# Last output chunk's rounding behind the last convolution's boundary, relation stage's first tables read in the gated block, root sums around the low parts

## The chip, the cores and the metric

The program runs on one core of one Trainium2 chip. TensorE (PE in the rows) multiplies, VectorE (DVE), ScalarE (ACT) and GpSimd (POOL) do the rest, and SyncE (SP) and ScalarE's own queue start DMAs. The engines run side by side and meet only at semaphores; each takes its own instructions in the order in which they are written. The metric is the device time of the whole program in microseconds (us), as a median of runs; lower is better.

## What is computed

Four layers on 256 nodes of 768 features, each a graph part and a feed-forward part added to the node stream x. The change lies in the gated feed-forward part of layer 2 (eight experts, one chosen) and in layer 3: a relational graph convolution, a plain one behind it, and a feed-forward part with two of eight experts. All data is fp32.

```python
# layer 3, graph part (x is already normalised)
agg  = segment_sum(x[src], edge_type * n + dst, 34 * n)
cnt  = segment_sum(ones,   edge_type * n + dst, 34 * n)
mean = agg.reshape(34, n, -1) / maximum(cnt, 1).reshape(34, n, 1)
h1   = einsum('rni,rio->no', mean, W_rel) + x @ W_root + b_rgcn
xw   = h1 @ W_gcn
out  = segment_sum(xw[src] * norm, dst, n) + xw * dinv**2 + b_gcn     # added to x
# layer 3, feed-forward part (on the normalised x)
probs  = softmax(x @ Wr + br); weights of the two largest, scaled to sum 1
h      = gelu(x @ W1[e] + b1[e]) for 8 experts
out    = sum_e weight_e * (h_e @ W2[e] + b2[e]); layer norm; added to x
```

## The kernel before, in words

**Precision by parts.** An fp32 product is made of three passes of TensorE: hi*hi, lo*hi and hi*lo. So every weight chunk that SyncE loads into `w_in` is first rounded by ScalarE into `w_hi` (`high`, `high_chunk`), and then VectorE writes the remainder into `w_lo` (`low`, `low_chunk`, through `low_of`). Both buffers have two halves, used in turn; each chunk goes in two parts p = 0 and 1, of three row tiles each. `w_in` has one buffer for each p: SyncE starts the load of the next chunk's part p when ScalarE and VectorE have both counted the part before (`w_high[p]`, `w_low[p]`). TensorE waits for `w_low` (`chunk`, `weights`).

**A boundary.** Between two parts the stream x is updated from PSUM, its statistics are taken (`stats_of`), it is scaled into `xn` (the memory of `neg_b`), TensorE turns it (`turn_tile`), ScalarE rounds the turned tile (`evict_tile`, with the square root of the variance before it in `deviation`) and VectorE writes its remainder (`low_tile`). There are two tiles m = 0 and 1 of 128 nodes. `boundary` does this for the convolutions' outputs, `tile_by_tile` is ScalarE's side of it.

**The gated block and the relation stage.** In the gated block of layer 2, ScalarE rounds and VectorE lowers the chunk C_ROOT, VectorE adds the block's output to x (`gated_out`), and the boundary to the relation stage follows. TensorE multiplies by `W_root` (`product` into REL_BANKS, tiles 0 and 1). Then, for each of 34 relations, a 256x256 table of edge counts is read from HBM into `ct` (the memory of `scores_b`) by a DMA on ScalarE's queue (`load_counts`, two half buffers). VectorE clips it into `REL_C[half]`, which is `aT_hi` or `aT_lo` (`counts`, semaphore `r_count`). TensorE forms the transposed means out of it (`mean`, banks 3 to 5), ScalarE rounds these (`round_means`, semaphore `r_high`), VectorE writes the remainder (`mean_low`, semaphore `r_low`: `hid_lo` for even relations, `xT_lo` for odd ones), and TensorE multiplies by the relation's weights (`relation`). The product of the relation before lies in the same banks, so `relation` waits for `r_acc`, which VectorE counts when it has taken a tile's sum out: `root(m)` for the root product, `accumulate(r, m)` for a relation. TensorE's order at the entry is: root product of tile 0, of tile 1, `mean(0, 0)`, seven filling matmuls (`idle`), `relation(0)`.

**The last convolution.** `gcn(1)` multiplies by `W_gcn` and aggregates; VectorE's `gcn_out(1)` is the boundary 8 behind it. TensorE then turns tile 0, multiplies by the chunk C_FFN3, scores the router (8 columns wide) and goes on. The chunks C_FFN3 + 1 and + 2 (`ffn_out` in the rows, 97 partitions) are needed only by the last products.

**What sets the order.** Nothing is planned by a tool: each engine's program is written by hand in the order in which it runs. So an instruction that stands too early in a list holds back all that stands behind it.

Of the kernel before, what the change touches and what calls it, by code (L numbers as in the profile page):

```python
# [16 lines left out]
P = 128  # L17
N = 256
# [43 lines left out]
def gnn_ffn_kernel(nc, t):  # L62

    ctx = ExitStack()
    with ctx:
# [180 lines left out]
        def flat(ap):  # L246
            return ap.rearrange("p a b -> p (a b)")
# [616 lines left out]
        def _(act):  # L864
# [243 lines left out]
            high_chunk(C_ROOT)  # L1108
            for m in range(M):
                act.wait_ge(*((f_mm[2], 5) if m == 0 else (w_used, used(C_FFN2 + 2))))  # L1110
                for (b, c0, c1, o) in NODE_BANKS[m]:
                    keep(outb[:, m, o:o + c1 - c0], bank[b][:, c0:c1], f_act[2])
                if m == 0:
                    deviation(0)
# [4 lines left out]
            act.wait_ge(e_added, 16 * ET + 16)  # L1119

            def load_counts(r, half):
                act.dma_start(ct[:, half, :, :], table[bass.ds(r * N, N), :].rearrange("(m p) n -> p m n", p=P))\
                   .then_inc(ld_ct[half], 16)

            load_counts(0, 0)
            load_counts(1, 1)
# [33 lines left out]
            high_chunk(C_FFN3 + 1)  # L1160


            tile_by_tile(8)
            act.wait_ge(f_dve[3], 1)
# [11 lines left out]
        def _(dve):  # L1176
# [418 lines left out]
            low_chunk(C_ROOT)  # L1595
            dve.wait_ge(x_type, 1)
# [16 lines left out]
            biased(3)  # L1613
            dve.wait_ge(x_high, 1)
            low_of(h_lo[:, :, :], xn[:, :, :], h_hi[:, :, :], x_low)

            def counts(half, landed):

                dve.wait_ge(ld_ct[half], landed)
                ts(flat(REL_C[half][:, :, :]), flat(ct[:, half, :, :]), EXACT, ALU.min).then_inc(r_count, 1)  # L1620
# [33 lines left out]
            counts(0, 16)  # L1654
            low(nth(C_REL), 0)
            mean_low(0, 0)
            counts(1, 16)
            for m in range(M):
                root(m)
                dve.wait_ge(r_acc, m + 1)  # L1660
            low(nth(C_REL) + 1, 1)
            accumulate(0, 0)
            mean_low(1, 1)
            with dve.Fori(1, REL // 2) as i:
                for half in range(2):
                    r = i * 2 + half
                    counts(half, i * 16 + 16)
                    dve.wait_ge(r_acc, r * 2 - 1)
                    accumulate(r - 2, 1)
                    low(r + nth(C_REL), half)  # L1670
                    accumulate(r - 1, 0)
                    mean_low(r, half)
# [19 lines left out]
            low_chunk(C_FFN3 + 1)  # L1692
            gcn_out(1)


            route(3)
# [82 lines left out]
```

## Time and profile before

| | us |
|---|---|
| median of 3 runs | 1414.98 (1413.61 to 1418.78) |
| the profiled execution | 1413.81 |
| its span, from the first to the last instruction | 1412.0 |
| TensorE matmul busy | 1307.5 (93%) |
| VectorE busy | 1004.7 (71%) |
| ScalarE busy | 627.4 (44%) |
| mean granted clock of TensorE | 0.981 of 2.4 GHz |

Times in rows are counted from the first instruction of the span. A row of the timeline has the start, the duration (of several merged instructions together), the engine, the line, what is written and read, and in brackets the idle time ahead of it and who ended it. An engine that ends in q is the engine's queue, which starts DMAs. A busy TensorE is not TensorE at full speed: its clock is granted at 2.4 or 1.2 GHz (1.00 or 0.50 in the rows).

### The profile page before, as it was taken

The numbers are of one execution on the slowest core, as the hardware profiler recorded it, in microseconds if no ns is written. First come the engines' busy times: TensorE is split into PE (matmuls) and PEld (weight loads), VectorE is DVE, ScalarE is ACT, GpSimd is POOL, SyncE is SP. The second block draws the span as 40 slices with busy tenths as digits, with TensorE's granted clock in tenths as the row PEclk, the third lists the DMA queues.
The fourth block names the chain that finished last, engine by engine and source line by source line (L and its number), as shares of the span: only waits on it lengthen the run. The fifth ranks groups of instructions, "written<-read, shape, count | busy, mean of one in ns | idle before, by whom it ended". The sixth has DMA issues, their size and how long they took to land.

```text
span 1412.0 us, 21374 instructions
## 1 busy us (share of the span) xinstructions
PE 1307.5 (93%) x7833; PEld 1145.5 (81%) x7833; DVE 1004.7 (71%) x1677; ACT 627.4 (44%) x795; POOL 216.0 (15%) x160
## 2 busy tenths in 40 slices
PE   5799999997899999997899999999999999999876
PEld 4499999974689999976677788888898889889765
DVE  7888888877798888876857756665665566566555
ACT  2256665544355665543444434333433333343421
POOL 0033444331024334440000000000000000002000
PEclk9999999998999999999999999999999999999988
DMA  9465556653266655643334544454445445434610
GB/s 345 147 200 195 163 163 191 202 132 92 87 194 200 184 163 164 201 148 112 116 109 156 192 181 149 159 199 162 149 178 193 149 150 195 175 141 146 197 36 23
DMA packets 103718, 227.32 MB, mean 161 GB/s; under 512 B 16688, under 2 KB 34672, under 8 KB 103684
## 3 DMA queue, kind: packets, MB, share of 16 engines
q1 hardware_dynamic: 72780, 192.43, 38.5%
q10 hardware_dynamic: 20968, 31.78, 8.0%
q0 software_dynamic: 9936, 2.66, 1.9%
q8 instruction: 20, 0.33, 0.1%
q14 instruction: 14, 0.11, 0.0%
HBM read 216.56 MB, written 10.29 MB: 161 GB/s over the span
## 4 chain that ended last, share of the span: by engine, by line
PE 63%; DVE 24%; issue 8%; ACT 3%; DMA 1%; DVEq 1%; ACTq 0%; SPq 0%
PE bank L418 61%; DVE w_lo L1181 6%; DVE hid_lo L1181 2%; DVE h_lo L1181 2%; DVE neg_b L1325 1%; DVE scores_b L1276 1%; DVE stats L1219 1%; ACT w_hi L892 1%; DVE scores_b L1278 1%; DVE scores_b L1187 1%; ACT z_b L960 1%; PE bank L457 1%; PE bank L514 1%; DVE same L1299 1%; DVE spare L1394 1%
## 5 line engine op out<-in xcount | busy, mean ns | idle before, releaser
L1181 DVE TENSOR_TENSOR w_lo<-w_in,w_hi 128x2304 fp32r<-128x2304 f32 (+4 forms) x162 | 396.5, 2476 | 61.4 <-ACT w_hi L892 61.3
L892 ACT ACTIVATE w_hi<-w_in 128x2304 fp32r<-128x2304 f32 (+4 forms) x162 | 328.4, 2062 | 234.7 <-PE bank L418 197.2
L418 PE MATMUL bank<-w_hi,xT_hi 128*128 128x384 f32 (+3 forms) x942 | 323.4, 343 | 7.0 <-DVE xT_lo L1181 4.5
L418 PE MATMUL bank<-w_lo,xT_hi 128*128 128x384 f32 (+3 forms) x942 | 308.8, 340 | 0.0
L418 PE MATMUL bank<-w_hi,hid_hi 128*128 128x512 f32 (+2 forms) x858 | 294.6, 343 | 9.0 <-DVE hid_lo L1181 3.5
L418 PE MATMUL bank<-w_lo,hid_hi 128*128 128x512 f32 (+2 forms) x858 | 272.5, 338 | 0.0
L418 PE MATMUL bank<-w_hi,xT_lo 128*128 128x384 f32 (+3 forms) x942 | 247.3, 341 | 0.0
L418 PE MATMUL bank<-w_hi,hid_lo 128*128 128x512 f32 (+2 forms) x858 | 225.2, 339 | 0.0
L418 PEld LDWEIGHTS bank<-w_hi,xT_hi 128*128 128x128 f32 (+1 forms) x942 | 178.2, 189 | 36.4 <-issue 8.9
L418 PEld LDWEIGHTS bank<-w_hi,hid_hi 128*128 128x128 f32 (+1 forms) x858 | 162.3, 189 | 45.5 <-issue 4.7
L1641 DVE SCALAR_TENSOR_TENSOR neg_b<-bank,rinv,neg_b 128x512 f32<-128x512 f32 (+1 forms) x136 | 77.5, 611 | 157.5 <-PE bank L418 157.5
L418 PEld LDWEIGHTS bank<-w_lo,xT_hi 128*128 128x128 f32 (+1 forms) x942 | 177.9, 189 | 13.8 <-issue 0.8
L418 PEld LDWEIGHTS bank<-w_lo,hid_hi 128*128 128x128 f32 (+1 forms) x858 | 162.5, 189 | 18.9
L377 POOL DMA_INDIRECT table<-value,row_i x64 | 121.6, 1899 | 255.1 <-DMA table<-value,row_i 236.7
L418 PEld LDWEIGHTS bank<-w_hi,xT_lo 128*128 128x128 f32 (+1 forms) x942 | 157.2, 190 | 2.4 <-issue 0.8
L418 PEld LDWEIGHTS bank<-w_hi,hid_lo 128*128 128x128 f32 (+1 forms) x858 | 134.7, 191 | 1.0
L418 PE MATMUL bank<-aT_hi,h_hi 128*128 128x256 f32 (+1 forms) x408 | 106.4, 280 | 2.7 <-DVE aT_lo L1181 2.7
L418 PE MATMUL bank<-aT_hi,h_lo 128*128 128x256 f32 (+1 forms) x408 | 106.7, 283 | 0.0
L418 PE MATMUL bank<-aT_lo,h_hi 128*128 128x256 f32 x396 | 103.9, 281 | 0.0
L892 ACT ACTIVATE xT_hi<-bank 128x512 fp32r<-128x512 f32 (+1 forms) x87 | 46.6, 554 | 119.5 <-PE bank L418 65.2
L403 POOL DMA_INDIRECT w_in<-L_gnn_W_rel,xrow_i x6 | 7.3, 1212 | 531.0 <-DVE w_lo L1181 529.5
L1187 DVE CUSTOM_DVE_ANT_0 spare<-z_b,a_bc 128x768 f32<-128x768 f32 x72 | 69.0, 958 | 20.6 <-ACT z_b L892 12.4
(225 smaller groups left out, 1565.2 us busy)
## 6 DMA issues: line engine op xcount, KB each, us to landing
w_in<-L_gnn_W_rel SPq DMA_DIRECT2D x68, 1152.0 KB, 5.6
w_in<-L_gnn_W SPq DMA_DIRECT2D x66, 1152.0 KB, 5.7
table<-zrow SPq DMA_DIRECT2D x1, 9216.0 KB, 36.2
scores_b<-table ACTq DMA_DIRECT2D x34, 256.0 KB, 2.9
a_bc<-L_gnn_a_src ACTq DMA_DIRECT2D x18, 384.0 KB, 3.8
a_bc<-L_gnn_a_dst ACTq DMA_DIRECT2D x18, 384.0 KB, 5.3
key_row<-key_rows ACTq DMA_DIRECT2D x16, 256.0 KB, 5.5
w_in<-ffn_out SPq DMA_DIRECT2D x4, 864.0 KB, 7.0
```

The source lines that it names most:

```text
L377: pool.indirect_dma_start(out=cells, out_offset=bass.IndirectOffsetOnAxis(ap=row_i[:, g:g + 1], axis=0), in_=value[:, g:g + 1], in_offset= ...
L418: return pe.matmul(out, lhsT, rhs, start=start, stop=stop, **kw)
L457: last = pe.transpose(bank[TURNED[i][m][half]][:, k * P:(k + 1) * P], xn[:, m, (3 * half + k) * P:(3 * half + k + 1) * P], ident[:, :])
L514: last = pe.transpose(bank[7][:, sm * N + m * P:sm * N + (m + 1) * P], alpha[:, m, sm * P:(sm + 1) * P], ident[:, :])
L892: act.activation(out, ps, func, **kw).then_inc(mark, 1)
L960: last = act.activation(z_b[:, k, :], bank[(5, 3, 4)[j]][:, (k % 2) * N:(k % 2 + 1) * N], ACT.Identity, bias=b1_head[:, k:k + 1])
L1181: return dve.tensor_tensor(out, a, b, op)
L1187: return dve.tensor_tensor_reduce(out=out, in0=a, in1=b, scale=1.0, scalar=0.0, op0=op0, op1=op1, accum_out=acc)
L1219: last = dve.bn_stats(stats[:, m, j, :], x_sb[:, m, j * HALF:(j + 1) * HALF])
L1276: last = dve.scalar_tensor_tensor(score[:, m, :], bank[7][:, 0:N], scal[:, 2 + m:3 + m], mask[:, m, :], add_, add_)
L1278: step(dve.scalar_tensor_tensor(flat(leaky[:, :, :]), flat(score[:, :, :]), 0.2, flat(score[:, :, :]), mul, mx))
L1641: last = dve.scalar_tensor_tensor(xs, bank[b][:, c0:c1], weight, xs, mul, add_)
```

## The change

Three groups of instructions move within the lists of ScalarE and VectorE; TensorE's and SyncE's lists stay as they are, and no instruction is added or removed.

1. ScalarE reads the first two count tables behind the rounding of C_ROOT instead of behind `h_hi`, and VectorE clips both directly behind the remainders of C_ROOT.
2. At the entry of the relation stage VectorE does `root(0)` ahead of the first relation's weight remainders and `root(1)` behind them, ahead of `mean_low(0, 0)`; `biased(3)`, which adds a bias to x, moves behind `mean_low(1, 1)`.
3. ScalarE rounds C_FFN3 + 1 behind both tiles of boundary 8, and VectorE lowers it behind `gcn_out(1)`.

```diff
@@ ScalarE
             high_chunk(C_ROOT)
+            act.wait_ge(e_added, 16 * ET + 16)
+            def load_counts(r, half):
...
+            load_counts(0, 0)
+            load_counts(1, 1)
...
             keep(h_hi[:, :, :], xn[:, :, :], x_high)
-            act.wait_ge(e_added, 16 * ET + 16)
...
-            load_counts(0, 0)
-            load_counts(1, 1)
...
-            high_chunk(C_FFN3 + 1)
             tile_by_tile(8)
+            high_chunk(C_FFN3 + 1)
@@ VectorE
             low_chunk(C_ROOT)
+            counts(0, 16)
+            counts(1, 16)
             dve.wait_ge(x_type, 1)
...
             low_tile(6, 1)
-            biased(3)
             dve.wait_ge(x_high, 1)
             low_of(h_lo[:, :, :], xn[:, :, :], h_hi[:, :, :], x_low)
...
-            counts(0, 16)
+            dve.wait_ge(x_low, 1)
+            root(0)
             low(nth(C_REL), 0)
+            root(1)
             mean_low(0, 0)
-            counts(1, 16)
-            for m in range(M):
-                root(m)
-                dve.wait_ge(r_acc, m + 1)
+            dve.wait_ge(r_acc, 2)
             low(nth(C_REL) + 1, 1)
             accumulate(0, 0)
             mean_low(1, 1)
+            biased(3)
...
             gcn_low(1)
+            gcn_out(1)
             low_chunk(C_FFN3 + 1)
-            gcn_out(1)
             route(3)
```

VectorE's list at the entry of the relation stage, before: behind the last tile's remainder come the two bias additions, `h_lo`, the first clipped table (`aT_hi`), the remainders of the first relation's weights, those of its means, the second table, and the root sums (`neg_b` from `hbias_bc`).

```order
L1181 TENSOR_TENSOR x_sb<-x_sb,bias_bc 128x768 [waits ld_bias]
L1181 TENSOR_TENSOR x_sb<-x_sb,bias_bc 128x768
L1181 TENSOR_TENSOR h_lo<-neg_b,h_hi 128x1536 [waits x_high,dve_step]
L1184 TENSOR_SCALAR aT_hi<-scores_b 128x512 [waits ld_ct0]
L1181 TENSOR_TENSOR w_lo<-w_in,w_hi 128x2304 [waits w_high_0]
L1181 TENSOR_TENSOR w_lo<-w_in,w_hi 128x2304 [waits w_high_1]
L1181 TENSOR_TENSOR hid_lo<-bank,hid_hi 128x512 [waits rel_high] x3
L1184 TENSOR_SCALAR aT_lo<-scores_b 128x512 [waits ld_ct1]
L1181 TENSOR_TENSOR neg_b<-bank,hbias_bc 128x512 [waits rel_out]
L1181 TENSOR_TENSOR neg_b<-bank,hbias_bc 128x256
L1181 TENSOR_TENSOR neg_b<-bank,hbias_bc 128x512 [waits w_used,rel_acc]
L1181 TENSOR_TENSOR neg_b<-bank,hbias_bc 128x256
```

The same place of the changed kernel.

```order
L1181 TENSOR_TENSOR h_lo<-neg_b,h_hi 128x1536 [waits x_high]
L1181 TENSOR_TENSOR neg_b<-bank,hbias_bc 128x512 [waits rel_out,x_low]
L1181 TENSOR_TENSOR neg_b<-bank,hbias_bc 128x256
L1181 TENSOR_TENSOR w_lo<-w_in,w_hi 128x2304 [waits w_high_0]
L1181 TENSOR_TENSOR w_lo<-w_in,w_hi 128x2304 [waits w_high_1]
L1181 TENSOR_TENSOR neg_b<-bank,hbias_bc 128x512 [waits w_used]
L1181 TENSOR_TENSOR neg_b<-bank,hbias_bc 128x256
L1181 TENSOR_TENSOR hid_lo<-bank,hid_hi 128x512 [waits rel_high] x3
```

The root sums stand ahead of the mean's remainders, the two tables have left the stretch, and so have the bias additions.

ScalarE's list in the gated block, as a piece of the difference: `w_hi` is the rounding of C_ROOT, `spare` takes the block's output from PSUM.

```order
 L892 ACTIVATE w_hi<-w_in 128x2304 [waits w_full_0,w_used]
 L892 ACTIVATE w_hi<-w_in 128x2304 [waits w_full_1]
+L1112 DMA scores_b<-table 128x2x256 [waits e_added]
+L1112 DMA scores_b<-table 128x2x256
 L892 ACTIVATE spare<-bank 128x512 [waits ffn2_mm]
 L892 ACTIVATE spare<-bank 128x256
```

The two table reads now stand between the last rounding of C_ROOT and the first eviction of the block's output.

ScalarE's list at boundary 8, as a piece of the difference: `std` and `xT_hi` are the boundary's two tiles, the rows of 97 partitions the chunk C_FFN3 + 1.

```order
 L892 ACTIVATE rw_hi<-rw 128x48 [waits ld_mid]
+L892 ACTIVATE std<-mv 128x1 [waits ln_var]
+L892 ACTIVATE xT_hi<-bank 128x3x128 [waits ln_t] x2
+L892 ACTIVATE std<-mv 128x1 [waits ln_var]
+L892 ACTIVATE xT_hi<-bank 128x3x128 [waits ln_t] x2
 L892 ACTIVATE w_hi<-w_in 97x2304 [waits w_row_0,w_full_0,w_used]
 L892 ACTIVATE w_hi<-w_in 97x2304 [waits w_row_1,w_full_1]
```

The boundary's six activations stand ahead of the chunk's two roundings; on VectorE the chunk's two remainders go in the same way from ahead of the boundary's first `x_sb` to behind its last `xT_lo`, ahead of the router's first instruction.

## Rows read from the trace of the kernel before

**Rows 1.** Timeline, VectorE, from the gated block's end to the relation stage's entry.
```profile
752.26 5.03 DVE L1181 TENSOR_TENSOR w_lo<-w_in,w_hi 128x2304 fp32r<-128x2304 f32 x2 [1.22 <-ACT w_hi L892]
...
769.21 1.82 DVE L1181 TENSOR_TENSOR x_sb<-x_sb,bias_bc 128x768 f32<-128x768 f32 x2
771.06 1.76 DVE L1181 TENSOR_TENSOR h_lo<-neg_b,h_hi 128x1536 fp32r<-128x1536 f32 x1
...
776.08 5.03 DVE L1181 TENSOR_TENSOR w_lo<-w_in,w_hi 128x2304 fp32r<-128x2304 f32 x2 [2.92 <-ACT w_hi L892]
781.02 1.88 DVE L1181 TENSOR_TENSOR hid_lo<-bank,hid_hi 128x512 fp32r<-128x512 f32 x3
782.82 0.41 DVE L1184 TENSOR_SCALAR aT_lo<-scores_b 128x512 fp32r<-128x512 f32 x1
783.15 2.07 DVE L1181 TENSOR_TENSOR neg_b<-bank,hbias_bc 128x512 f32<-128x512 f32 x4
```

**Rows 2.** Timeline, TensorE, same stretch: turn, root product, first mean, first relation.
```profile
761.05 0.87 PE L457 MATMUL bank<-ident,neg_b 128*128 128x128 f32 x6 [1.14 <-DVE neg_b L1184]
...
767.22 0.82 PE L457 MATMUL bank<-ident,neg_b 128*128 128x128 f32 x6
...
776.31 0.28 PE L418 MATMUL bank<-aT_hi,h_hi 128*128 128x256 f32 x1
...
784.22 0.50 PE L418 MATMUL bank<-w_hi,hid_hi 128*128 128x512 f32 x1 [3.34 <-DVE neg_b L1181]
```

**Rows 3.** Timeline, ScalarE and its queue, same stretch.
```profile
768.08 0.39 ACTq L1122 DMA_DIRECT2D scores_b<-table  x1
...
768.50 1.49 ACT L892 ACTIVATE h_hi<-neg_b 128x1536 fp32r<-128x1536 f32 x1
...
773.92 4.15 ACT L892 ACTIVATE w_hi<-w_in 128x2304 fp32r<-128x2304 f32 x2 [3.92 <-DVE aT_hi L1184]
...
779.39 0.60 ACT L892 ACTIVATE hid_hi<-bank 128x512 fp32r<-128x512 f32 x1 [0.35 <-PE bank L418]
```

**Rows 4.** Table reads: time from issue to landing of all 34.
```profile
DMA to landing us min/median/max: 2.6/2.9/4.3
```

**Rows 5.** Stretches: length, busy time (count) by engine, granted clock, DMA share, GB/s.
```profile
785.80:788.80 3.00, 3.00 (x11) 2.52 (x10) 2.49 (x1) 2.15 (x2) 0.00 (x0) 0.50 0.43 154
...
1354.40:1359.40 5.00, 4.99 (x17) 3.85 (x18) 2.96 (x7) 1.07 (x3) 0.00 (x0) 0.52 0.02 3
```

**Rows 6.** Timeline, VectorE, one turn of the relation loop.
```profile
817.17 1.14 DVE L1641 SCALAR_TENSOR_TENSOR neg_b<-bank,rinv,neg_b 128x512 f32<-128x512 f32 x2 [4.78 <-PE bank L418]
```

**Rows 7.** Timeline, VectorE, behind the last convolution.
```profile
1347.53 2.56 DVE L1181 TENSOR_TENSOR w_lo<-w_in,w_hi 97x2304 fp32r<-97x2304 f32 x1 [1.06 <-ACT w_hi L892]
1350.00 1.14 DVE L1544 SCALAR_TENSOR_TENSOR x_sb<-bank,dinv,x_sb 128x512 f32<-128x512 f32 x2
```

**Rows 8.** Timeline, TensorE, behind the last convolution.
```profile
1343.48 1.90 PE L418 MATMUL bank<-zero 128*128 128x512 bf16 x8
1354.41 1.54 PE L457 MATMUL bank<-ident,neg_b 128*128 128x128 f32 x6 [9.03 <-DVE neg_b L1184]
...
1362.04 0.82 PE L457 MATMUL bank<-ident,neg_b 128*128 128x128 f32 x6
```

**Rows 9.** Timeline, VectorE and TensorE, behind layer 2's convolution.
```profile
716.09 1.14 DVE L1544 SCALAR_TENSOR_TENSOR x_sb<-bank,dinv,x_sb 128x512 f32<-128x512 f32 x2 [1.29 <-PE bank L418]
...
716.94 1.90 PE L418 MATMUL bank<-zero 128*128 128x512 bf16 x8
720.50 0.88 PE L457 MATMUL bank<-ident,neg_b 128*128 128x128 f32 x6 [1.66 <-DVE neg_b L1184]
```

**Rows 10.** Timeline, ScalarE and VectorE, boundary 8's second tile, router, hidden sums.
```profile
1362.57 0.88 ACT L892 ACTIVATE xT_hi<-bank 128x384 fp32r<-128x384 f32 x2 [6.00 <-PE bank L457]
...
1368.90 0.17 DVE L1181 TENSOR_TENSOR lg<-bank,rb 128x16 f32<-128x16 f32 x1 [4.79 <-PE bank L418]
...
1376.87 1.02 DVE L1181 TENSOR_TENSOR z_b<-bank,hbias_bc 128x512 f32<-128x512 f32 x2 [1.93 <-PE bank L418]
```

More of the change, by code:

```diff
@@ L1108, in _ @@
             high_chunk(C_ROOT)
+            act.wait_ge(e_added, 16 * ET + 16)
+            def load_counts(r, half):
+                act.dma_start(ct[:, half, :, :], table[bass.ds(r * N, N), :].rearrange("(m p) n -> p m n", p=P))\
+                   .then_inc(ld_ct[half], 16)
+            load_counts(0, 0)
+            load_counts(1, 1)
             for m in range(M):
@@ L1118, in _ @@
             keep(h_hi[:, :, :], xn[:, :, :], x_high)
-            act.wait_ge(e_added, 16 * ET + 16)
-            def load_counts(r, half):
-                act.dma_start(ct[:, half, :, :], table[bass.ds(r * N, N), :].rearrange("(m p) n -> p m n", p=P))\
-                   .then_inc(ld_ct[half], 16)
-            load_counts(0, 0)
-            load_counts(1, 1)
             def round_means(r, half, more):
@@ L1159, in _ @@
             keep(rw_hi[:, :], rw[:, :], rw_high)
+            tile_by_tile(8)
             high_chunk(C_FFN3 + 1)
-            tile_by_tile(8)
             act.wait_ge(f_dve[3], 1)
@@ L1595, in _, with counts @@
             low_chunk(C_ROOT)
+            def counts(half, landed):
+                dve.wait_ge(ld_ct[half], landed)
+                ts(flat(REL_C[half][:, :, :]), flat(ct[:, half, :, :]), EXACT, ALU.min).then_inc(r_count, 1)
+            counts(0, 16)
+            counts(1, 16)
             dve.wait_ge(x_type, 1)
@@ L1612, in _ @@
             low_tile(6, 1)
-            biased(3)
             dve.wait_ge(x_high, 1)
             low_of(h_lo[:, :, :], xn[:, :, :], h_hi[:, :, :], x_low)
-            def counts(half, landed):
-                dve.wait_ge(ld_ct[half], landed)
-                ts(flat(REL_C[half][:, :, :]), flat(ct[:, half, :, :]), EXACT, ALU.min).then_inc(r_count, 1)
             def excess(landed):
```

## The prediction

> **What bounds the kernel now.** The first look is at the table of busy shares: TensorE works for 93% of the span and its list is unchanged, so time can only come out of stretches in which TensorE waits or runs at the lower clock. The second look is at the timeline of the two places that the change touches. At the entry of the relation stage TensorE has finished the first mean and its filling matmuls, then idles 3.34 us until VectorE's `neg_b`, the root sums [rows 2]. VectorE works without a break in that time: 5.03 us of weight remainders, 1.88 us of mean remainders, a table, 2.07 us of root sums [rows 1]. Behind the last convolution TensorE idles 9.03 us [rows 8]; there VectorE sits in front of the remainders of C_FFN3 + 1, whose last part ends at 1350.09, and only then does the boundary begin, at 1350.00 (the starts of neighbours overlap a little) [rows 7]. The third look is at the granted clock in both places: after each of the two waits it reads about one half for a while, 0.50 over 3.0 us and 0.52 over 5.0 us [rows 5]. So each wait costs twice: once as idle time, once as slow matmuls behind it.
>
> **The change part by part**, with times of the profiled execution.
>
> *Tables in the gated block.* VectorE clips both tables directly behind the remainders of C_ROOT, which end at 757.29 [rows 1]. One takes 0.41 us, and its follower starts 0.33 us after it [rows 1], so the two cost about 0.7 us. VectorE is the engine that TensorE waits for in the boundary that follows (1.14 us at 761.05 [rows 2]), so nothing hides this: **+0.7 us** for all that comes behind, the root product and the first mean included. The tables must have landed by 757.29. ScalarE's queue runs ahead of its engine: a read that is written behind `h_hi` was issued at 768.08, while `h_hi` started at 768.50 [rows 3]. In the gated block the read stands behind a rounding that waits for the root weights; VectorE's first remainder starts at 752.26 and the second rounding soon after, so I put the issue at 752.6 and 753.1. Landing takes 2.6 to 4.3 us [rows 4]: the second table is there between 755.7 and 757.4. I take the median, 2.9, so no wait; the upper end costs 0.1 us, and a read that has to share with the weights' load might add 1 us. The Trainium skill, DMA: Bandwidth & Descriptors, section Issuing engines are not separate DMA queues, says that reads started by ScalarE interleave with SyncE's on the same 16 engines, which speaks against reading tables where weights stream in; by it the landing would tend to the upper end, and the sum would lose those tenths. ScalarE itself pays for the issues in its queue only, not in its engine.
>
> *Relation entry.* With the 0.7 us the first mean starts at 777.0 instead of 776.31 [rows 2]. Before, ScalarE began its last rounding of the mean 3.08 us after that start (779.39 [rows 3]). Now: 780.1, 0.60 us long, 0.3 us to VectorE, 0.7 us for the last remainder, which makes **781.7**. The other path to the same point is VectorE's own list. `h_hi` ends at 770.0 + 0.7 [rows 3]; `h_lo` takes 1.76, `root(0)` half of 2.07, the weight remainders 5.03, `root(1)` 1.04, the mean remainders 1.88 [rows 1]: with 0.2 for the first hand-over this gives 781.6. The weight remainders are not late any more: ScalarE's rounding of them was held until 773.92 by the wait for the first table [rows 3], which stood behind the biases (1.82 us) and `h_lo` (1.76 us) on VectorE [rows 1]; the table is now clipped long before, so the rounding starts right behind `h_hi`, at 770.7, and the first part is done at 772.8, before VectorE asks for it at 773.7. `root(1)` asks at 778.7 for a product that is done at 777.0. So TensorE starts `relation(0)` at 781.7 instead of 784.22: **-2.5 us**, the 0.7 paid already. The filling matmuls now end about there, so the gap of 3.34 us shrinks to some tenths.
>
> *The clock behind it.* Without the gap I expect the clock to stay at 1.00, as it does after the gap of 1.14 us at 761.05. The 3.0 us at 0.50 [rows 5] then take 1.5: **-1.5 us**.
>
> *Biases.* 1.82 us [rows 1], now between `mean_low(1, 1)` and the loop, where VectorE has 4.78 us of idle time in each turn [rows 6]. What is queued behind is the clipping of relation 2's table, needed only a product later. **0 us.** The same slack of 4.78 us says that the loop is bound by TensorE, so what the entry gains goes through all 34 relations unchanged.
>
> *Boundary 8.* In layer 2 the same convolution has no rounding ahead of its boundary: VectorE starts on the sum 0.85 us before the first filling matmul behind the aggregation (716.09 against 716.94 [rows 9]). Here these fillers start at 1343.48 [rows 8], so VectorE can start at 1342.6 instead of 1350.00: **-7.4 us**. From there to the turn it takes 4.41 us in both layers (1350.00 to 1354.41, 716.09 to 720.50 [rows 7 to 9]), and nothing else becomes late: VectorE and ScalarE have nothing left ahead of it. TensorE's gap is then 1.7 us as in layer 2 [rows 9] instead of 9.03.
>
> *The clock behind that.* From the turn of tile 0 to that of tile 1 TensorE took 7.63 us here (1354.41 to 1362.04 [rows 8]) and 6.17 us for the same instructions in boundary 6 (761.05 to 767.22 [rows 2]), where the clock had stayed up: **-1.5 us**.
>
> *Where the rounding goes.* ScalarE rounds behind `xT_hi` of tile 1, which ends at 1363.45 [rows 10]; 2.1 us for the first part (half of 4.15 [rows 3]), 0.3 to VectorE, two remainders in 5.0 us: 1370.9 in the old times, against 1368.90 for the router's first instruction [rows 10]. The router's chain is 2.0 us late. But behind it VectorE waited 1.93 us for TensorE before the hidden sums of tile 1 [rows 10]: the lateness takes this wait's place, and **+0.1 us** is left. The last chunk's load starts later too, but its rounding stands behind the hidden sums of 1376.87 [rows 10].
>
> **The sum**: -2.5 - 1.5 - 7.4 - 1.5 + 0.1 = -12.8 us. The profiled execution would take 1413.81 - 12.8 = 1401.0, the median 1414.98 - 12.8 = 1402.2. A measurement of this kernel can tell about 0.5%, 7 us, from no change.
>
> **The rivals.**
>
> *The clock falls all the same.* The gaps of 1.7 us at boundary 8, of 1.8 us now at boundary 6, or what is left at the relation entry might bring it down in one or two places, or the router's narrow matmuls might do it longer than before. For it: there is one row at 1.7 us, in layer 2, and none at 1.8 in boundary 6. Against: in that row the clock stayed up. Price: 1.5 us for each place, so **1403.7 to 1405.2**. The Trainium skill, TensorE: Matmul & The Clock Gate, Part 1: The HAM clock gate, says that the monitor runs on without regard to the kernel, so the point at which the clock changes moves from run to run; by that rule a shift of the whole stream alone can win or lose such a stretch.
>
> *The rounding that was moved becomes the wait.* If ScalarE comes to the chunk late, or the two remainders take the router's place by more than the 1.93 us of slack, each us beyond is lost one to one: the whole of the 5.0 us of remainders less 1.93 is the most that this can take, 3.1 us, **1405.3**.
>
> *It doesn't do what it says at boundary 8.* If VectorE can't start on the sum before 1350 for another reason (the sum's banks, ScalarE), only the entry's 4.0 us are left: **1411**. Layer 2's rows speak against it.
>
> *Slower.* The relation loop starts at another phase against the loads of weights and tables, and the turn, bound by TensorE so far, becomes bound by VectorE's or the loads' chain. It decides from 12.8 / 33 = 0.39 us a turn; at 0.6 us a turn the time is 1402.2 + 33 x 0.6 = **1422**. Against it: all waits in the loop hang on the turn itself, with 4.78 us to spare [rows 6].
>
> **How the numbers follow.** The forecast, 60%: 1402.2, from 1400.5 to 1403.5. The clock falls in one or two places, 22%. The rounding becomes the wait, 10%. Only the entry gains, 4%. Slower, 2%; the last 2% is left to gains beyond the sum, such as a stretch of low clock behind the router that goes too. The range must also hold the spread of the runs, 1413.61 to 1418.78 for the kernel before, so it goes from 1399.0 to 1406.5. Faster by over 0.5% needs 1407.9 or less: 0.94. Within 0.5%: 0.04. Slower: 0.02.
>
> **What would show it.** In the timeline of the changed kernel: two clippings of 0.4 us directly behind the remainders of C_ROOT with no wait for a DMA ahead of them; a gap of TensorE before the first relation under 1 us and a clock of 1.00 over the 10 us behind it; the turn of boundary 8 about 3.5 us behind the start of the eight filling matmuls instead of 10.9; the two remainders of 97 partitions ahead of the router's first instruction; and VectorE's wait ahead of the second hidden sum gone. It would be wrong if VectorE showed a wait for a table, if the clock read 0.50 in either place, or if the loop's turn were no longer the same length.

## The result, and the profile after

| | before | after |
|---|---|---|
| median, same chip | 1416.25 us (1413.61 to 1419.41, 6 runs) | 1405.49 us (1403.43 to 1407.49, 6 runs) |
| ratio | | 0.9914, 95% interval 0.9901 to 0.9928 |
| profiled execution | 1413.81 us | 1407.49 us |
| its span | 1412.0 us | 1405.7 us |
| granted clock, mean | 0.981 | 0.980 |

The changed kernel is faster by 10.8 us in the medians. The forecast was 12.8 us and 1402.2, counted from a median of 1414.98 before; more runs of the kernel before put that at 1416.25. The two medians alone give a ratio of 0.9924, inside the interval.

The two spans differ by 6.3 us only, and yet the change was worth more than that. VectorE's remainders of C_ROOT, its last work that is the same in both kernels, start at 752.26 before [rows 1] and at 755.70 after. Instructions are the same up to there; what differs is TensorE's granted clock in some stretches. One of them, in the kernel before and then in the changed one (columns as in [rows 5]):

```profile
704.00:707.40 3.40, 3.40 (x21) 3.01 (x20) 3.37 (x4) 3.40 (x5) 0.00 (x0) 1.00 0.59 119
```

```profile
704.00:707.40 3.40, 3.40 (x13) 2.82 (x12) 3.37 (x5) 3.34 (x4) 0.00 (x0) 0.50 0.51 119
```

TensorE is busy all the time in both, with 21 matmuls in one and 13 in the other. Over all traces of this study whose code is the same up to there, C_ROOT's remainders start anywhere from 751.93 to 757.10. So from here on two traces are compared from that start, called R below, and not by their spans. From R to the end the kernel before takes 659.74 us and the changed one 649.98: the change is worth **9.8 us in the trace**. R has an uncertainty of its own: in some traces the second half of `W_root` lands a little later, and all behind R with it, by up to 0.4 us.

The entry of the relation stage, VectorE of the changed kernel (timeline), answers to [rows 1]:

```profile
755.70 5.03 DVE L1181 TENSOR_TENSOR w_lo<-w_in,w_hi 128x2304 fp32r<-128x2304 f32 x2 [1.22 <-ACT w_hi L892]
760.65 0.42 DVE L1184 TENSOR_SCALAR aT_hi<-scores_b 128x512 fp32r<-128x512 f32 x1
760.98 0.42 DVE L1184 TENSOR_SCALAR aT_lo<-scores_b 128x512 fp32r<-128x512 f32 x1
...
775.93 1.02 DVE L1181 TENSOR_TENSOR neg_b<-bank,hbias_bc 128x512 f32<-128x512 f32 x2
776.87 5.01 DVE L1181 TENSOR_TENSOR w_lo<-w_in,w_hi 128x2304 fp32r<-128x2304 f32 x2
781.80 1.01 DVE L1181 TENSOR_TENSOR neg_b<-bank,hbias_bc 128x512 f32<-128x512 f32 x2
782.73 2.09 DVE L1181 TENSOR_TENSOR hid_lo<-bank,hid_hi 128x512 fp32r<-128x512 f32 x3
```

Both clippings stand behind the remainders with no bracket, so no wait for a table: the two reads were issued at 756.0 and 756.4 and landed 2.7 and 2.9 us later, over a microsecond ahead of the clippings. The wait of 2.92 us ahead of the relation's weight remainders [rows 1] is gone. TensorE, same stretch, answers to [rows 2]:

```profile
765.17 0.88 PE L457 MATMUL bank<-ident,neg_b 128*128 128x128 f32 x6 [1.81 <-DVE neg_b L1184]
...
780.42 0.28 PE L418 MATMUL bank<-aT_hi,h_hi 128*128 128x256 f32 x1
...
783.30 1.68 PE L418 MATMUL bank<-zero 128*128 128x512 bf16 x7
785.16 0.49 PE L418 MATMUL bank<-w_hi,hid_hi 128*128 128x512 f32 x1 [0.17 <-issue]
```

The idle time ahead of `relation(0)` fell from 3.34 to 0.17 us. Boundary 8, TensorE with VectorE's first sum among it, answers to [rows 7] and [rows 8]:

```profile
1338.57 0.57 PE L418 MATMUL bank<-h_hi,cntT_hi 128*128 128x512 f32 x1 [1.82 <-DVE h_lo L1181]
...
1343.57 1.14 DVE L1544 SCALAR_TENSOR_TENSOR x_sb<-bank,dinv,x_sb 128x512 f32<-128x512 f32 x2 [4.03 <-PE bank L418]
...
1344.42 1.90 PE L418 MATMUL bank<-zero 128*128 128x512 bf16 x8
1347.99 0.88 PE L457 MATMUL bank<-ident,neg_b 128*128 128x128 f32 x6 [1.66 <-DVE neg_b L1184]
...
1354.07 0.82 PE L457 MATMUL bank<-ident,neg_b 128*128 128x128 f32 x6
```

The gap of 9.03 us is 1.66. Stretches of the changed kernel: behind `relation(0)`, the last aggregation, the turn of boundary 8, and behind the router.

```profile
784.20:794.20 10.00, 9.83 (x63) 8.44 (x62) 7.19 (x6) 5.39 (x4) 0.00 (x0) 1.00 0.69 248
...
1338.60:1344.50 5.90, 5.90 (x25) 4.96 (x26) 1.87 (x4) 0.00 (x0) 0.00 (x0) 0.71 0.92 215
...
1344.40:1354.00 9.60, 7.43 (x42) 5.21 (x41) 6.29 (x15) 1.16 (x4) 0.00 (x0) 1.00 0.00 0
...
1359.30:1366.10 6.80, 6.80 (x28) 6.22 (x28) 6.00 (x19) 2.98 (x4) 0.00 (x0) 0.50 0.30 88
```

Both low stretches of [rows 5] are at 1.00 now. Two others took part of the gain: the last aggregation at 0.71, which the kernel before did at 1.00, and a longer low stretch behind the router. The aggregation in the kernel before, timeline and stretch:

```profile
1339.16 0.50 PE L418 MATMUL bank<-h_hi,cntT_hi 128*128 128x512 f32 x1 [1.80 <-DVE h_lo L1181]
```

```profile
1339.20:1345.10 5.90, 5.90 (x32) 4.32 (x32) 2.13 (x3) 2.13 (x1) 0.00 (x0) 1.00 0.83 201
```

The same gap of 1.8 us stands ahead of it in both kernels; in one the clock fell behind it, in the other not.

Marks from R, in us, for the kernel before and the changed one:

| from R to | before | after | difference | so far forecast |
|---|---|---|---|---|
| turn of boundary 6 | 8.79 | 9.47 | +0.68 | +0.7 |
| `relation(0)` | 31.96 | 29.46 | -2.50 | -2.5 |
| the next mean, behind `relation(0)` | 39.89 | 35.86 | -4.03 | -4.0 |
| last aggregation | 586.90 | 582.87 | -4.03 | -4.0 |
| turn of boundary 8, tile 0 | 602.15 | 592.29 | -9.86 | -11.4 |
| the same, tile 1 | 609.78 | 598.37 | -11.41 | -12.9 |
| turn of the hidden values (`spare` by `ident`), behind router and hidden sums | 629.21 | 619.44 | -9.77 | -12.8 |
| end | 659.74 | 649.98 | -9.76 | -12.8 |

### The profile page after: what moved, and what is told of

The parts are those of the page before. It is cut to its first block, busy times and chain, and to the rows that moved or that the text cites. A ratio compares the mean times of both kernels' runs of the same rounds, so it can differ in the third digit from the quotient of the medians.

```text
span 1405.7 us, 21373 instructions
## 1 busy us (share of the span) xinstructions
PE 1310.6 (93%) x7833; PEld 1149.2 (82%) x7833; DVE 1004.6 (71%) x1677; ACT 627.4 (45%) x795; POOL 217.0 (15%) x160
## 4 chain that ended last, share of the span: by engine, by line
PE 61%; DVE 24%; issue 8%; ACT 4%; DMA 1%; DVEq 1%; ACTq 0%; SPq 0%
PE bank L418 59%; DVE w_lo L1181 6%; DVE hid_lo L1181 2%; DVE h_lo L1181 2%; DVE neg_b L1325 1%; ACT w_hi L892 1%; DVE scores_b L1276 1%; DVE stats L1219 1%; DVE scores_b L1278 1%; ACT z_b L960 1%; DMA w_in<-L_gnn_W 1%; DVE scores_b L1187 1%; PE bank L457 1%; DVE same L1299 1%; PE bank L514 1%
```

## The experiments

The question that the traces leave: is each term what the prediction says, and are the 3 us that are missing in the last table lost to the clock or to the moved rounding? The rival says that the rounding, which now stands ahead of the router, costs them. Every kernel below computes the whole; filling matmuls multiply zeros and add nothing to the result.

**The halves.** The entry alone is the changed kernel with boundary 8 as before:

```diff
 ScalarE                          VectorE
+high_chunk(C_FFN3 + 1)          +low_chunk(C_FFN3 + 1)
 tile_by_tile(8)                  gcn_out(1)
-high_chunk(C_FFN3 + 1)          -low_chunk(C_FFN3 + 1)
```

> The changes at the gated block and at the relation entry alone; boundary 8 as before. My theory: two independent places, whose gains add. The first relation starts 2.5 us earlier, measured from the start of C_ROOT's remainders (31.96 before, 29.5 now), the clock behind it stays at 1.00 (1.5 us), boundary 8 keeps its wait of 9.0 us: 2.5 to 4.0 us faster, ratio 0.9972 to 0.9982. Rival (one place is swallowed by the other, or the gain of the entry is given back in the relation loop): ratio 1.000, with a turn of the loop longer than 15.51 us.

Measured: 1415.07 us, ratio 0.9986 (0.9974 to 0.9998). `relation(0)` starts at R + 31.38, only 0.58 earlier than before, and not the expected 2.5. From the turn of boundary 6 it is 21.53 against 19.99 in the changed kernel, and 1.5 of this stand between the root product and the first mean (14.91 us here, 13.38 before). Timeline of TensorE and the stretch behind it:

```profile
764.72 0.88 PE L457 MATMUL bank<-ident,neg_b 128*128 128x128 f32 x6 [2.55 <-DVE neg_b L1184]
```

```profile
766.80:770.10 3.30, 3.30 (x11) 2.82 (x11) 2.10 (x6) 0.20 (x1) 0.00 (x0) 0.50 0.02 5
```

The clock fell during the root product, behind the turn's gap of 2.55 us. The turn itself is 0.38 later than in the changed kernel, R + 9.85, because the second half of `W_root` landed later. The mean behind `relation(0)` is at R + 37.78, 2.11 earlier than before: the 4.03 of the changed kernel less 1.5 for the low stretch and 0.4 for the turn. Behind the loop 0.6 us of this are lost again: the clock fell in the last aggregation, and the turn of boundary 8 comes 15.57 us behind the aggregation's start instead of 15.25.

The other half is the kernel before with only the boundary's edits:

```diff
 ScalarE                          VectorE
-high_chunk(C_FFN3 + 1)          -low_chunk(C_FFN3 + 1)
 tile_by_tile(8)                  gcn_out(1)
+high_chunk(C_FFN3 + 1)          +low_chunk(C_FFN3 + 1)
```

> The change at boundary 8 alone. My theory: TensorE's wait there falls from 9.0 to 1.7 us, 7.4 us faster, and 1.5 us more by the clock: 7.4 to 8.9 us, ratio 0.9937 to 0.9948, and with e1_entry's gain it makes the whole of the change. Rival (the remainders that now stand ahead of the router's first instruction cost up to 3.1 us): 4.3 us or more, ratio 0.997, with no wait of VectorE left ahead of the second hidden sum.

Measured: 1411.65 us, 0.9959 (0.9946 to 0.9973). From the last aggregation to the turn 7.88 us instead of 15.25: -7.37, the term of -7.4. The next turn follows 6.08 instead of 7.63 us later: -1.55. And then 1.6 us are lost behind the router, as in the changed kernel (18.27 us from the router's first matmul to the turn of the hidden values, 16.68 before). In the timeline VectorE waits ahead of the second hidden sum as long as before [rows 10], where the forecast had said that this wait would be gone; the stretch shows why:

```profile
1374.30 1.02 DVE L1179 TENSOR_TENSOR z_b<-bank,hbias_bc 128x512 f32<-128x512 f32 x2 [1.99 <-PE bank L418]
```

```profile
1363.50:1370.30 6.80, 6.80 (x25) 6.12 (x26) 5.93 (x21) 2.61 (x3) 0.00 (x0) 0.50 0.32 88
```

TensorE is busy for all of it, at 0.50. VectorE waits for a slow TensorE, not TensorE for the late rounding.

**Parts of the entry.** The tables alone are read and clipped in the gated block; roots and biases stay:

```diff
 ScalarE:  high_chunk(C_ROOT)
+          load_counts(0, 0); load_counts(1, 1)
 VectorE:  low_chunk(C_ROOT)
+          counts(0, 16); counts(1, 16)
```

> Only the first two tables are read and clipped in the gated block; root sums and bias additions stay where they were. By VectorE's list: the clippings cost 0.7 us ahead of the boundary, the weights' rounding is no longer held by a table, and the root sums behind the mean's remainders still hold TensorE: first relation 30.6 us behind the start of C_ROOT's remainders (31.96 before, 29.5 with the whole change), a gain of 1.4 us. Rival (the table held nothing of the path): 0.7 us later than before.

Measured: 1415.67 us, 0.9986 (0.9971 to 1.0002), which can't be told from no change by the median. By the trace, from the turn to `relation(0)` 20.61 instead of 23.17 us; less 0.68 for the clippings ahead of the turn, this is -1.9 us. From R it starts at 30.46 (expected 30.6). TensorE in the timeline:

```profile
787.56 0.50 PE L418 MATMUL bank<-w_hi,hid_hi 128*128 128x512 f32 x1 [0.81 <-DVE neg_b L1181]
```

The gap is 0.81 and the relation behind it runs at full clock: 6.42 us to the next mean instead of 7.93.

The counterpart moves `root(0)`, `root(1)` and `biased(3)` and leaves the tables:

```diff
-biased(3)
 low_of(h_lo, xn, h_hi)
 counts(0, 16)
+root(0)
 low(nth(C_REL), 0)
+root(1)
 mean_low(0, 0)
...
 mean_low(1, 1)
+biased(3)
```

> Only the order at the entry: biases behind the second mean's remainders, root sums around the weight remainders; both tables are read and clipped where they were. By VectorE's list: the rounding of the weights still waits for the first table, now clipped 1.8 us earlier for want of the biases; first relation 31.2 us behind the start of C_ROOT's remainders, a gain of 0.7 to 0.8 us. Rival (the root sums are the whole of the wait): 29.9 us, a gain of 2.1 us.

Measured: 1416.54 us, 0.9988 (0.9971 to 1.0004). From the turn to `relation(0)` 22.07 us, -1.1; from R 31.24, as expected (31.2), and not the rival's 29.9. VectorE still waits for the weights' rounding, which the first table's clipping still holds back, and TensorE still waits for the mean's remainders:

```profile
777.12 5.03 DVE L1181 TENSOR_TENSOR w_lo<-w_in,w_hi 128x2304 fp32r<-128x2304 f32 x2 [2.00 <-ACT w_hi L892]
```

```profile
785.21 0.49 PE L418 MATMUL bank<-w_hi,hid_hi 128*128 128x512 f32 x1 [2.29 <-DVE hid_lo L1181]
```

With a gap of 2.29 the relation is slow (7.99 us). So each part alone helps, and in these traces only the ones with the tables moved have a gap small enough (1.00 us or less) that the clock stays.

Back in the changed kernel, the biases return to their old place:

```diff
 low_tile(6, 1)
+biased(3)
 low_of(h_lo, xn, h_hi)
...
 mean_low(1, 1)
-biased(3)
```

> The changed kernel with the two bias additions (1.82 us) back in their old place ahead of h_lo. By VectorE's list: h_lo waited 0.73 us for ScalarE in the changed kernel, so 1.82 - 0.73 = 1.1 us reach the list, and the first relation starts 0.8 to 1.1 us later than in the changed kernel (30.3 to 30.6 us). Rival (another path is as long): 29.5 us, no loss.

Measured: 1406.56 us, 0.9924 (0.9901 to 0.9946). `relation(0)` starts 0.84 us later (20.83 against 19.99 from the turn), as expected, with a gap of 1.00, and the relation is fast (6.40):

```profile
783.58 0.49 PE L418 MATMUL bank<-w_hi,hid_hi 128*128 128x512 f32 x1 [1.00 <-DVE hid_lo L1181]
```

All the same this trace ends at R + 649.20, 0.8 us before the changed kernel's: the aggregation stayed at full clock (1.5 us less) and so did more of the part behind the router (1.6 us less), while the product behind boundary 8's turn was slow (7.63 instead of 6.08 us). The clock's stretches are worth more than this part of the change.

**The price of the clippings ahead of the boundary.** In the changed kernel both move behind the scaling of the boundary's second tile:

```diff
 low_chunk(C_ROOT)
-counts(0, 16); counts(1, 16)
...
 scaled(1)
+counts(0, 16); counts(1, 16)
 low_tile(6, 1)
```

> The changed kernel with the two clippings moved from ahead of the boundary to behind the scaling of its second tile, where VectorE waits 2.7 us for ScalarE. My theory (the clippings sit on the path ahead of the boundary and cost 0.66 us there): the turn of boundary 6 and all behind it come 0.66 us earlier, the first relation 28.8 us behind the start of C_ROOT's remainders; ratio 0.0005 below the changed kernel's, which only the traces can show. Rival (something else sets the boundary): no difference in the trace.

Measured: 1407.14 us, 0.9929 (0.9906 to 0.9952). The turn is at R + 8.80 and `relation(0)` at R + 28.79, both 0.67 earlier than in the changed kernel. Timeline: the turn, and the clippings and the remainders behind them, which wait for ScalarE:

```profile
763.85 0.88 PE L457 MATMUL bank<-ident,neg_b 128*128 128x128 f32 x6 [1.13 <-DVE neg_b L1184]
```

```profile
768.28 0.42 DVE L1184 TENSOR_SCALAR aT_hi<-scores_b 128x512 fp32r<-128x512 f32 x1
768.62 0.42 DVE L1184 TENSOR_SCALAR aT_lo<-scores_b 128x512 fp32r<-128x512 f32 x1
...
771.06 1.02 DVE L1181 TENSOR_TENSOR xT_lo<-bank,xT_hi 128x384 fp32r<-128x384 f32 x2 [2.02 <-ACT xT_hi L892]
```

Ahead of these remainders VectorE waits for ScalarE in any case: 2.69 us in the changed kernel, and 2.02 here, where the clippings fill the rest. So they cost nothing there. That shows the +0.7 as a real price at their present place. A median can't show 0.67 us.

**What the clock gives back by itself.** If the waits cost a second time through the clock, then filling them with matmuls, and leaving their lengths, should give back that part alone. The kernel before, with the waits filled:

```diff
-idle(7, 7)
+idle(7, 21)
...
-turn_tile(8, 0, 8)
+turn_tile(8, 0, 48)
```

> The kernel before with more filling matmuls in the two waits of TensorE and nothing else changed: 21 instead of 7 ahead of the first relation, 48 instead of 8 ahead of boundary 8's turn. The waits for VectorE stay. My theory (a wait costs twice, as idle time and as slow matmuls behind it): the first relation and the turn start at the same distance as before, but the clock behind them reads 1.00; 3.0 us faster, ratio 0.998. Rival (the clock falls by the phase of the stream, not by these gaps): it reads 0.50 behind them as before, ratio 1.000.

Timeline of TensorE, the relation's start and the two turns of boundary 8:

```profile
786.25 0.50 PE L418 MATMUL bank<-w_hi,hid_hi 128*128 128x512 f32 x1 [0.33 <-DVE neg_b L1181]
...
1355.52 0.88 PE L457 MATMUL bank<-ident,neg_b 128*128 128x128 f32 x6 [0.97 <-DVE neg_b L1184]
...
1361.61 0.82 PE L457 MATMUL bank<-ident,neg_b 128*128 128x128 f32 x6
```

`relation(0)` starts as late as before from the turn (23.16 us), and its product takes 6.43 instead of 7.93; from turn to turn at boundary 8 it takes 6.09 (1361.61 - 1355.52) instead of 7.63. So in this trace the low clock behind the two waits went with the idle time, 1.5 us each. From R to the end it is 2.06 us shorter, and not 3.0: the turn of boundary 6 came 0.4 us later, where the second half of `W_root` landed later, and at boundary 8 the last chunk's load took 7.15 us instead of 6.59, so that the turn comes 0.6 us later behind the aggregation. But the timed runs say 1416.2 us, 1.0003 (0.9991 to 1.0014): at most 1.3 us faster (0.0009 x 1416). The expected gain is not in the median. The profiled run was the fastest of twelve, with the highest granted clock, 0.985; their median has 0.982 (1416.2 us), and the slowest 0.978 (1420.14 us). Where the other executions ran slowly no trace shows; that stays open.

Now the changed kernel itself, twice more, unchanged:

> The changed kernel again, unchanged. My theory: the waits are the same to 0.1 us, and the profiled executions differ in where the clock is at 0.50 in the boundaries with gaps of 1.6 to 1.9 us (in the first trace: ahead of the change and in the last aggregation). Expected: first relation 29.5 us behind the start of C_ROOT's remainders, turn of boundary 8 3.6 us behind the start of the fillers; total of the 0.50 stretches not the same as in the first trace; ratio 0.990 to 0.993. Rival (the low clock in the last aggregation and the longer one behind the router are caused by the change): they are in this trace at the same places again.

> The changed kernel a third time. My theory: the low stretch in the aggregation again, 9.4 us from its first matmul to the turn; ratio 0.9925, some 2 us above e11_aggfill2. Rival (chance): 7.9 us in this trace, and no difference between the two medians.

Measured: 1406.8 us, 0.9939 (0.9922 to 0.9956), and 1408.38 us, 0.9931 (0.9909 to 0.9953). The first of these repeats lies on the changed kernel's trace to within 0.03 us at nearly every mark, low stretches included, and ends at R + 649.96. That is what the rival had said, and not the expectation. The second repeat has some low stretches elsewhere. Its stretches, the last aggregation and the product behind boundary 8's turn:

```profile
1339.90:1345.80 5.90, 5.88 (x25) 4.98 (x26) 1.87 (x4) 0.00 (x0) 0.00 (x0) 0.71 0.91 208
...
1350.80:1354.20 3.40, 3.06 (x9) 2.61 (x10) 1.41 (x4) 0.08 (x1) 0.00 (x0) 0.50 0.02 5
```

The aggregation is slow again, now the turn's product is too (7.49 us instead of 6.09), and in exchange the part behind the router isn't (16.68 us instead of 18.31). It ends at R + 649.76, the same to 0.2 us.

So is the low clock in the aggregation a side effect of the change? The gap of 1.8 us ahead of it stands in eleven traces. In the five whose relation entry is that of the changed kernel (its three traces, the entry alone, the clippings late) the clock fell behind it. In the other six (before, boundary alone, tables alone, roots and biases alone, waits of before filled, biases back) it stayed. Chance alone would hardly sort them so. What in the entry does it, its shift of the stream or something else, no run separates.

To see what the aggregation's gap of 1.8 us is worth, seven more filling matmuls go into it in the changed kernel:

```diff
-idle(AGG_BANKS[1][0][0], 0 if sm else 2)
+idle(AGG_BANKS[1][0][0], 0 if sm else (9 if s else 2))
```

> The changed kernel with 9 instead of 2 filling matmuls ahead of the last aggregation, nothing else. My theory: TensorE's gap of 1.82 us there shrinks to 0.3, the clock reads 1.00 over the aggregation, the end of the aggregation comes 1.5 us earlier. Rival (the position of the stream against the monitor sets it, not this gap): the stretch of 0.50 is in the aggregation all the same or comes in the boundary right behind it.

Measured: 1404.47 us, 0.9907 (0.9885 to 0.9929). Timeline of TensorE ahead of the aggregation and at the second turn, VectorE at the router and the second hidden sum, and the stretch of the aggregation:

```profile
1337.07 0.50 PE L418 MATMUL bank<-h_hi,cntT_hi 128*128 128x512 f32 x1 [0.31 <-DVE h_lo L1181]
...
1351.03 0.82 PE L457 MATMUL bank<-ident,neg_b 128*128 128x128 f32 x6
...
1359.42 0.17 DVE L1181 TENSOR_TENSOR lg<-bank,rb 128x16 f32<-128x16 f32 x1
...
1365.86 1.02 DVE L1181 TENSOR_TENSOR z_b<-bank,hbias_bc 128x512 f32<-128x512 f32 x2 [0.41 <-PE bank L418]
```

```profile
1337.10:1343.00 5.90, 5.90 (x32) 4.32 (x32) 3.34 (x8) 0.00 (x0) 0.00 (x0) 1.00 0.89 213
```

The aggregation is at 1.00, from it to the turn 7.88 us instead of 9.42, and the part behind the router takes 16.68 us. This trace ends at R + 646.77, 12.97 us before the kernel before: the forecast's sum, in a trace in which the clock did what the forecast assumed, with seven matmuls that the change doesn't have. It also settles whether the rounding's lateness reaches TensorE. The router's first sum comes 8.39 us behind the turn of tile 1 (1359.42 - 1351.03), before 6.86 (1368.90 [rows 10] less 1362.04 [rows 8]): the moved rounding makes it 1.53 us late. The second hidden sum comes 14.83 us behind that turn in both (1365.86 - 1351.03, 1376.87 - 1362.04): the wait of 1.93 us has shrunk to 0.41 and taken all of it up.

Whether the moved rounding draws out the low stretch behind the router is another question. The part from the router's first matmul to the turn of the hidden values takes 16.7 us in all five traces with the old order. Of the nine with the new order it takes 18.2 to 18.3 in four (the changed kernel's first two, the boundary alone, the nine waits filled) and 16.7 in five. In those four the low stretch begins 2.5 to 3.6 us behind the router's first matmul and lasts 6.8 us, in the ten others it begins 4.0 to 5.2 us behind it and lasts 3.5. So the new order doesn't force the longer stretch; whether it makes it likelier, five traces of the old order can't tell.

The same kernel again:

> e10_aggfill once more, on one chip with e12_again2. My theory (the gap of 1.8 us, not chance, makes the low stretch in the aggregation): none in the aggregation, 7.9 us from its first matmul to boundary 8's turn; ratio to before 0.9905. Rival (chance from trace to trace): low in some traces whatever the fillers.

Measured: 1407.79 us, 0.9926 (0.9902 to 0.9951), beside 1408.38 us for the changed kernel on the same chip, 0.6 us and not the expected 2. Stretches: the root product, the aggregation, boundary 8's turn.

```profile
761.60:765.00 3.40, 3.40 (x13) 2.42 (x13) 2.84 (x6) 0.98 (x2) 0.00 (x0) 0.51 0.18 73
...
1335.70:1341.60 5.90, 5.85 (x32) 4.37 (x32) 3.35 (x8) 0.00 (x0) 0.00 (x0) 1.00 0.88 208
...
1345.30:1348.70 3.40, 3.27 (x10) 2.82 (x11) 1.19 (x3) 0.00 (x0) 0.00 (x0) 0.50 0.00 0
```

The aggregation stays at 1.00, but this time the clock fell behind two of the gaps that were left, of 1.84 and 1.66 us. The end is at R + 649.30. So in both traces filling one gap kept the clock up behind that gap, and it is no sure gain for the whole.

**Nine waits filled.** The clippings as in the kernel that moved them behind the scaling, and more filling matmuls in nine waits:

```diff
-idle(AGG_BANKS[1][0][0], 0 if sm else 2)
+idle(AGG_BANKS[1][0][0], 0 if sm else (9 if s else 2))
-turn_tile(3, 0, 4)   turn_tile(5, 0, 8)   turn_tile(6, 0, 3)   turn_tile(8, 0, 8)
+turn_tile(3, 0, 11)  turn_tile(5, 0, 14)  turn_tile(6, 0, 7)   turn_tile(8, 0, 14)
-gcn(0, 1, C_GCN2, 4, 3)    gcn(1, 1, C_GCN3, 7, 2)   idle(4, 14)
+gcn(0, 1, C_GCN2, 4, 11)   gcn(1, 1, C_GCN3, 7, 8)   idle(4, 20)
+idle(0, 8)
 pe.wait_ge(f_dve[3], 7)
```

> A version meant to beat both: the changed kernel with the clippings behind the second tile's scaling (as in e6_late) and with filling matmuls in TensorE's gaps of 1.6 to 2.2 us in the boundaries of layers 1 to 3, in the last aggregation and in the last part (11 for 4 at boundary 3, 11 for 3 at 4, 14 for 8 at 5 and 8, 7 for 3 at 6, 8 for 2 at 7, 9 for 2 ahead of the aggregation, 20 for 14 and 8 new ones in the last part). My theory (the gaps bring the clock down, wherever the monitor stands): the 0.50 stretches behind these gaps are gone from the trace, the one behind the router stays; 3 to 5 us faster than the changed kernel, ratio to before 0.989 to 0.991. Rival (the narrow matmuls and transposes bring it down, not the gaps): the stretches stay, ratio 0.9925.

Measured: **1400.21 us, 0.9870 (0.9845 to 0.9894)**, beside 1404.47 for the kernel with one gap filled on the same chip: the fastest of the study, and more than the expected 0.989 to 0.991. Timeline of TensorE, the turn of boundary 8:

```profile
1341.99 0.87 PE L457 MATMUL bank<-ident,neg_b 128*128 128x128 f32 x6 [0.36 <-DVE neg_b L1185]
```

From R to the end 646.49 us, with R at 751.55, the earliest of all. Not every gap is closed: 3.14 us are left ahead of the turn at 701.04, and the clock is low behind it. The low stretch behind the router is still there too, and long (18.22 us from the router to the turn of the hidden values). The part behind that turn, where the last of the new fillers stand, takes 28.99 instead of 30.53 us. Which of the other fillers gave how much was not tested one by one.

**Traces against medians.** The change of the time from R to the end, against what the ratio makes of 1416 us:

| kernel | trace, us | (ratio - 1) x 1416, us (interval) |
|---|---|---|
| changed | -9.8 | -12.2 (-14.0 to -10.2) |
| changed, first repeat | -9.8 | -8.6 (-11.0 to -6.2) |
| changed, second repeat | -10.0 | -9.8 (-12.9 to -6.7) |
| entry alone | -1.5 | -2.0 (-3.7 to -0.3) |
| boundary alone | -7.0 | -5.8 (-7.6 to -3.8) |
| tables alone | -3.1 | -2.0 (-4.1 to +0.3) |
| roots and biases alone | -0.9 | -1.7 (-4.1 to +0.6) |
| waits of before filled | -2.1 | +0.4 (-1.3 to +2.0) |
| biases back | -10.5 | -10.8 (-14.0 to -7.6) |
| clippings late | -10.6 | -10.1 (-13.3 to -6.8) |
| one gap filled, first | -13.0 | -13.2 (-16.3 to -10.1) |
| one gap filled, second | -10.4 | -10.5 (-13.9 to -6.9) |
| nine waits filled | -13.3 | -18.4 (-21.9 to -15.0) |

In the last row the trace column leaves out what the fillers ahead of R gave. The only other rows that disagree are the first, by 0.4 us beyond the interval's end, and the filled kernel before.

## Why the prediction was right, and where not

The forecast was that the change is faster by about 12.8 us; measured were 10.8 in the medians and 9.8 in the trace. The median, 1405.49, lies in the range of 1399.0 to 1406.5, but above the 1400.5 to 1403.5 that the forecast itself had named, and some luck is in that: two repeats on other chips gave 1406.8 and 1408.38. By its steps:

- *Tables in the gated block, +0.7.* Right: the turn of boundary 6 is 0.68 later, and 0.67 earlier again when the clippings move away. The tables had landed 2.7 and 2.9 us behind their issue, where the forecast took 2.9. The prediction's fear of a late landing, drawn from the Trainium skill (DMA: Bandwidth & Descriptors, section Issuing engines are not separate DMA queues: reads started by ScalarE and SyncE interleave on the same 16 engines), was not put to the test. `W_root` had landed when the two reads started (the DMA share is 0.00 from 756.0 to 757.0), and the next weights' load was issued at 758.48 only. So no run shows the 1 us that sharing was said to add.
- *Relation entry, -2.5.* Right to 0.01 us (-2.50). Both paths of the estimate were real: with the tables alone TensorE still waited for the root sums, with the roots alone for the mean's remainders, behind a weights' rounding that the first table still held back.
- *The clock behind it, -1.5.* Right: -1.53, at 1.00 over the 10 us behind. Filling the gap without shortening the wait gave the same 1.5 in the trace, so it goes with the idle time. In the medians of that kernel this gain doesn't appear.
- *Biases, 0, and the loop.* Right: VectorE's idle time in a turn is 4.78 us as before, and the 4.03 us from the entry stand unchanged ahead of the aggregation.
- *Boundary 8, -7.4.* Right in its mechanism. In the kernel before, the chain of waits that ends in this turn starts at the load of C_FFN3 + 1, which started at 1338.70 and landed at 1345.29, behind which both roundings stand; so a load, too, had held the boundary back. In the changed kernel VectorE starts on the sum 0.85 us ahead of the fillers (1343.57 against 1344.42), and the edit alone gave -7.37. In the changed kernel's traces 1.54 of it is missing, because the aggregation ahead ran slower.
- *The clock behind that, -1.5.* Right in the first trace (-1.54) and only in half of all. Of eight traces with the gap of 1.66 us, four show a low stretch behind it. That the first trace has none is luck.
- *The rounding that was moved, +0.1.* The size was right and the picture was not: the lateness is 1.5 us instead of 2.0, and the wait behind it takes up all. In the changed kernel's first profile this can't be seen, because TensorE was slow there for 1.6 us more (in the second repeat of the same kernel, where it wasn't, the wait is 0.42). The row that the forecast had named as its sign, the wait gone, reads 2.05:

```profile
1357.52 5.03 DVE L1181 TENSOR_TENSOR w_lo<-w_in,w_hi 97x2304 fp32r<-97x2304 f32 x2 [1.37 <-ACT w_hi L892]
1362.46 0.17 DVE L1181 TENSOR_TENSOR lg<-bank,rb 128x16 f32<-128x16 f32 x1
...
1370.54 1.02 DVE L1181 TENSOR_TENSOR z_b<-bank,hbias_bc 128x512 f32<-128x512 f32 x2 [2.05 <-PE bank L418]
```

The step that failed is the sum's silent assumption that all stretches which the change doesn't touch keep their clock. The first rival, "the clock falls all the same" in one or two places at 1.5 us each, with 1403.7 to 1405.2, is what the traces show: once in the aggregation (+1.54), once behind the router (+1.63), 3.2 us together. The forecast gave it 22%. It named the router as a place, and the gaps at the boundaries and at the relation entry; the aggregation's gap it didn't name, and in the trace of before the clock had stayed up behind it. The page of the Trainium skill that the prediction named for this rival (TensorE: Matmul & The Clock Gate, Part 1: The HAM clock gate: the monitor runs on without regard to the kernel) agrees with the second repeat of the changed kernel, where the same program has its low stretches at other instructions; the first repeat had them at the same ones.

The first comparison gave 12.2 us by its ratio and the two later ones 8.6 and 9.8. The granted clocks of the single runs go with this: three of the first six runs had 0.983 or 0.984 and took 1403.43 to 1404.21 us, of the twelve later ones a single run had that (0.984, 1402.92 us), the rest at most 0.981. Why so many of the first did stays open, and so does why the kernel before with filled waits gained nothing in its runs.

## What to carry to other kernels

Put work that nobody needs soon behind the chain that ends a stage, on every engine at once: the whole of the 7.4 us came from one chunk's rounding that stood one place too early in two lists. Of each wait that is closed, count the slow matmuls behind it as well, but as a gain that single runs may lose again elsewhere. Then look for all other gaps of the size of those here (1.7 to 2.5 us), for which one trace at full clock is no proof, fill them, and believe the medians: nine filled waits paid (0.987), two alone in the kernel before did not (1.0003). To size an edit, compare traces from the last common instruction ahead of it and not by span.

## What the runs showed of the hardware

- A gap of TensorE of 1.65 to 2.20 us, with filling matmuls ahead of it, sometimes brought the clock down and sometimes not. At four places (the turns of boundaries 6 and 8, `relation(0)`, the last aggregation) the 14 traces have 28 such gaps, and the clock fell at ten: at five of the eleven ahead of the aggregation, four of the eight at boundary 8, one of the nine at boundary 6. At the 20 gaps of 1.43 us or less it never fell, at the eight of 2.29 us or more always.
- TensorE at 100% busy is no sign that the clock stays up. The router's matmuls are 8 columns wide, and from the first of them TensorE was busy without a break. In every trace a low stretch began 2.5 to 5.2 us behind that first matmul. Its length (16.7 or 18.3 us from the router to the turn of the hidden values) decided 1.6 us of the result. That it is the narrow matmuls which bring the clock down was not tested.
- The same instructions ahead of R took from 751.93 to 757.10 us, 5.2 us or 0.4% of the kernel, and the low stretches lie at other places in them. That is more than the 4.0 us that the whole entry was worth.
